# GpSimd's queue no longer drained at block ends, one power for two, and single waits for x

## What is computed

```
x = x + 0.5 * _L0_ffn_ref(_layernorm(x, axis=-1), L0_ffn_router_w, ...)
x = x + _L0_attn_ref(_layernorm(x, axis=-1), ...)
x = x + 0.5 * _L0_ffn_ref(_layernorm(x, axis=-1), ...)
...
x = x + 0.5 * _L2_ffn_ref(_layernorm(x, axis=-1), L2_ffn_router_w, ...)
x = x + _L2_attn_ref(_layernorm(x, axis=-1), ...)
x = x + 0.5 * _L2_ffn_ref(_layernorm(x, axis=-1), ...)
...
```

```
logits = jnp.einsum('td,ed->te', xf, router_w)
top_vals, top_idx = jax.lax.top_k(logits, K)
probs = jax.nn.softmax(top_vals, axis=-1)
```

## Time and profile before

| | us |
|---|---|
| median of 3 runs | 3094.78 |
| lowest and highest | 3089.35, 3095.48 |
| span of the profiled execution | 3117.8 |
| PE busy | 2339.5 (75%) |
| DVE busy | 2080.5 (67%) |
| ACT busy | 1466.0 (47%) |
| POOL busy | 919.6 (29%) |

### The profile page before, as it was taken

How to read it: one execution, slowest core, us unless ns; L and a number is a source line. 1 busy time by engine, 2 the same in 40 slices (tenths; PEclk the granted TensorE clock), 3 DMA queues, 4 the chain that set the end, 5 groups by cost and what they waited for, 6 DMA issues and landing times. The chain is left out here.

```text
span 3117.8 us, 45115 instructions
## 1 busy us (share of the span) xinstructions
PE 2339.5 (75%) x13720; PEld 1448.2 (46%) x13720; DVE 2080.5 (67%) x5273; ACT 1466.0 (47%) x3122; POOL 919.6 (29%) x975
## 2 busy tenths in 40 slices
PE   2397688839857699999899976579584975677774
PEld 2397576738834222222222234479464873222223
DVE  3465777746644799999999924456574666576775
ACT  2265311116533388888888852156332654233232
POOL 4644234434412200010101004534254441121320
PEclk9999788869979799999999988689796996799998
DMA  4122100002220400000000000022201221000000
GB/s 144 43 65 73 34 8 14 14 26 62 59 68 14 149 17 19 19 17 19 19 19 18 9 29 21 29 54 63 68 31 40 62 82 47 0 0 0 0 0 27
DMA packets 111194, 115.74 MB, mean 37 GB/s; under 512 B 21904, under 2 KB 94192, under 8 KB 110192
## 3 DMA queue, kind: packets, MB, share of 16 engines
q1 hardware_dynamic: 92080, 71.64, 8.1%
q0 software_dynamic: 17408, 35.95, 3.4%
q10 hardware_dynamic: 1472, 5.27, 0.4%
HBM read 67.55 MB, written 44.83 MB: 36 GB/s over the span
## 5 line engine op out<-in xcount | busy, mean ns | idle before, releaser
L1732 DVE TENSOR_REDUCE attn_mx<-bank 128x1 f32<-128x512 f32 x1024 | 641.3, 683 | 59.9 <-PE bank L1511 51.9
L1633 ACT ACTIVATE attn_pT<-bank 128x512 f32<-128x512 f32 x1024 | 539.8, 604 | 126.2 <-PE bank L1526 125.8
L1511 PE MATMUL bank<-attn_K,attn_Q 48*128 48x512 bf16 x1024 | 336.5, 396 | 50.5 <-DVE attn_mx L1732 29.8
L1526 PE MATMUL bank<-attn_Q,attn_K 51*128 51x512 bf16 x1024 | 331.2, 386 | 2.4 <-ACT attn_pT L1633 1.6
L1539 PE MATMUL bank<-attn_pT,attn_vb 128*32 128x512 f32 x2048 | 275.8, 610 | 19.7 <-ACT attn_pT L1633 11.8
L1692 POOL TENSOR_TENSOR attn_m_rem<-attn_m_rem,attn_m_parts 8x128 f32<-8x128 f32 x128 | 53.3, 416 | 678.1 <-ACT attn_m_parts L1646 678.1
L1511 PEld LDWEIGHTS bank<-attn_K,attn_Q 48*128 48x128 bf16 x1024 | 71.8, 94 | 376.1 <-DVE attn_mx L1732 325.1
L2391 POOL TENSOR_TENSOR mix_rS<-mix_rT,mix_S 128x512 f32<-128x512 f32 x64 | 81.5, 1277 | 270.0 <-ACT mix_gT L2372 210.2
L903 PE MATMUL bank<-mix_prod_qk,ident 128*128 128x256 f32 x512 | 123.6, 396 | 0.9 <-issue 0.9
L903 PEld LDWEIGHTS bank<-mix_prod_qk,ident 128*128 128x128 f32 x512 | 102.5, 202 | 27.1 <-issue 13.3
L2325 PE MATMUL bank<-mix_rS,mix_sel 128*128 128x512 f32 x128 | 75.7, 680 | 41.8 <-POOL mix_rS L2391 41.8
(11 more groups left out here) (610 smaller groups left out, 5910.9 us busy)
## 6 DMA issues: line engine op xcount, KB each, us to landing
ffn0a_x_ring<-xs_rows SPq DMA_DIRECT2D x72, 65.0 KB, 1.8
ffn0b_x_ring<-xs_rows SPq DMA_DIRECT2D x72, 65.0 KB, 1.9
ffn2a_x_ring<-xs_rows SPq DMA_DIRECT2D x72, 65.0 KB, 1.8
ffn2b_x_ring<-xs_rows SPq DMA_DIRECT2D x72, 65.0 KB, 1.9
w<-in_L_w ACTq DMA_DIRECT2D x2, 2048.0 KB
ffn0a_y_back<-y_rows SPq DMA_DIRECT2D x8, 512.0 KB
ffn0b_y_back<-y_rows SPq DMA_DIRECT2D x8, 512.0 KB
w<-in_L_w SPq DMA_DIRECT2D x2, 2048.0 KB
```

The source lines that it names most:

```text
L1511: nc.tensor.matmul(a_bank[n % 3][:], slot(net.Q, h, 0, KROWS)[:, qt * P:(qt + 1) * P], slot(net.K, h, 0, KROWS)[:, hf * CH:(hf + 1) * CH], ...
L1526: nc.tensor.matmul(s_bank[n % 3][:], slot(net.K, h, 0, KROWS + MROWS)[:, kt * P:(kt + 1) * P], slot(net.Q, h, 0, KROWS + MROWS)[:, hf * CH ...
L1633: nc.scalar.activation(pT[:, kt % RING, hf * CH:(hf + 1) * CH], s_bank[(n * HPB + hf) % 3][:], ACT.Exp, scale=HD ** -0.5).then_inc(exp_rea ...
L1732: nc.vector.tensor_reduce(mx[:, h % 2, qt, hf:hf + 1], a_bank[n % 3][:], AX.X, ALU.max).then_inc(a_used, 1)
```

## The change

It has three parts, and they touch all blocks, three of the four routing stages (mix0 keeps its order), and the loads.

2. In the load stage, ffn1b and decay2 one power instruction of 128x8 values (`rstd_and_grow`) takes the place of two of 128x4: the deviation of chunk `c` and the gate of chunk `c - 1`. It waits for both of its inputs. In ffn1b and decay2 it is put amid the 8 scatters of a chunk (after 4 and after 6 of them), and in all three the last gate's power is put amid the scatters of chunk 6. Two memsets (`set_joint`) are added.
3. In the load stage each chunk of `x` has a semaphore of its own and is waited for when its turn comes. The layer-0 expert weights are issued by SyncE, behind `x` and the quantized weights, no longer by ScalarE.

```diff
-        return self.enter_context(self.nc.Block())
+        return self.enter_context(self.nc.Block(no_gpsimd_drain=True))
...
+    def set_joint(self, pool):
+        nc = self.nc
+        nc.gpsimd.memset(self.bases[:], float(np.e)).then_inc(self.joint_set, 1)
+        nc.gpsimd.memset(self.exponents[:], -0.5).then_inc(self.joint_set, 1)
+        pool.wait_ge(self.joint_set, 2)
+
+    def rstd_and_grow(self, pool, c):
+
+        pool.wait_ge(self.var_ready, c + 1)
+        pool.wait_ge(self.gap_ready, c)
+        need(pool, self.xn_ready, c)
+        need(pool, self.placed, c - 1)
+        self.nc.gpsimd.tensor_tensor(self.raised[:], self.bases[:], self.exponents[:], ALU.pow).then_inc(self.rstd_ready, 1)
...
+    def grow_last(self, pool):
+        c = NCH - 1
+        pool.wait_ge(self.gap_ready, c + 1)
+        need(pool, self.placed, c)
+        self.nc.gpsimd.tensor_tensor(self.ex[:], self.bases[:, 1, :], self.gap[:], ALU.pow).then_inc(self.rstd_ready, 1)
...
             for c in range(NCH):
-                sp.dma_start(dst[:, c * TPC:(c + 1) * TPC], src[:, c * TPC:(c + 1) * TPC]).then_inc(
-                    x_loaded if c else x_first, 16)
+                sp.dma_start(dst[:, c * TPC:(c + 1) * TPC], src[:, c * TPC:(c + 1) * TPC]).then_inc(x_loaded[c], 16)
...
             for t, src_w in quantized:
                 sp.dma_start(t[:], src_w).then_inc(int_loaded, 16)
+            for t, src_w in big:
+                sp.dma_start(t[:], src_w).then_inc(w_loaded, 16)
...
-            for dst, src in big:
-                act.dma_start(dst[:], src).then_inc(w_loaded, 16)
             steps(lambda c, depth: norm.keep(act, c), lambda c: None)
...
             def body(c, depth):
-                norm.rstd_pow(pool, c)
-                if depth > 0:
-                    norm.grow(pool, c - 1)
+                if depth == 0:
+                    norm.rstd_first(pool)
+                else:
+                    norm.rstd_and_grow(pool, c)
                 if depth > 1:
                     norm.scatter(pool, c - 2)

             def finish(c):
-                norm.grow(pool, c)
-                norm.scatter(pool, c - 1)
+                norm.scatter(pool, c - 1, range(0, 2))
+                norm.grow_last(pool)
+                norm.scatter(pool, c - 1, range(2, TPC))
                 norm.scatter(pool, c)
...
             def body(c, depth):
                 if depth > 1:
                     norm.place(dve, c - 2)
+                dve.wait_ge(x_loaded[c], 16)
                 norm.stats(dve, c)
...
-                if depth == 0:
-                    dve.wait_ge(x_loaded, 16 * (NCH - 1))
-                else:
+                if depth > 0:
                     norm.weigh(dve, c - 1)
```

GpSimd's program in ffn1b, and likewise in decay2 (there with `range(0, 3)` and `range(3, TPC)` in the loop):

```diff
-            def body(c):
-                norm.rstd_pow(pool, c)
-                if norm.route and c > 0:
-                    norm.grow(pool, c - 1)
-                    norm.scatter(pool, c - 1)
...
+            norm.set_joint(pool)
+            norm.rstd_first(pool)
+            norm.rstd_and_grow(pool, 1)
+            for c in range(2, NCH):
+                norm.scatter(pool, c - 2, range(0, 2))
+                norm.rstd_and_grow(pool, c)
+                norm.scatter(pool, c - 2, range(2, TPC))
+            norm.scatter(pool, NCH - 2, range(0, 2))
+            norm.grow_last(pool)
+            norm.scatter(pool, NCH - 2, range(2, TPC))
+            norm.scatter(pool, NCH - 1)
+            norm.all_scattered(pool)
```

More of the change, by code:

```diff
@@ L149, with __init__ @@
 class Norm:
-    def __init__(self, nc, st, net, tag, dest, route, across=False, settled=False):
-        self.across, self.settled = across, settled
+    def __init__(self, nc, st, net, tag, dest, route, across=False, settled=False, joint=False):
+        self.across, self.settled, self.joint = across, settled, joint
         def sb(name, shape, dt=F32):
@@ L164, in __init__ @@
         self.shift_ready = sem("shift_ready")
-        self.ve = sb("var_eps", [P, TPC])
-        self.rstd = sb("rstd", [P, TPC])
+        if joint:
+            self.bases, self.exponents, self.raised = (sb(k, [P, 2, TPC]) for k in ("bases", "exponents", "raised"))
+            self.ve, self.rstd, self.ex, self.gap = (
+                self.bases[:, 0, :], self.raised[:, 0, :], self.raised[:, 1, :], self.exponents[:, 1, :])
+            self.joint_set = sem("joint_set")
+        else:
+            self.ve = sb("var_eps", [P, TPC])
+            self.rstd = sb("rstd", [P, TPC])
+            if route:
+                self.ex, self.gap = sb("exp", [P, TPC]), sb("gap", [P, TPC])
         self.xn = sb("xn", [P, XRING, TOPK, TPC, XCOLS] if route else [P, CH])
@@ L190, in __init__ @@
             self.scattered = [sem(f"scattered{n}") for n in range(XRING)]
+            if joint:
+                self.grown = self.rstd_ready
     def view(self, t, c, width=D):
@@ L221, in stats @@
             need(dve, self.rstd_ready, c)
+        if self.joint and c == 0:
+            dve.wait_ge(self.joint_set, 2)
         nc.vector.tensor_scalar(self.ve[:], self.mv[:, :, 1], LN_EPS, None, ALU.add).then_inc(self.var_ready, 1)
@@ L296, in weigh @@
         rows = self.xn[:, c % XRING]
-        dve.wait_ge(self.grown, c + 1)
+        dve.wait_ge(self.grown, self.grown_count(c))
         own.then(nc.vector.tensor_scalar(self.den[:], self.ex[:], 1.0, None, ALU.add))
@@ L531, in load_stage @@
     with Scope(nc) as st:
-        norm = Norm(nc, st, net, "ln0", net.xnT[0], True)
-        x_first, x_loaded = st.sem("x_first_loaded"), st.sem("x_loaded")
+        norm = Norm(nc, st, net, "ln0", net.xnT[0], True, joint=True)
+        x_loaded = [st.sem(f"x_loaded{c}") for c in range(NCH)]
         first_loaded = st.sem("first_weights_loaded")
@@ L1132, in swiglu_stage @@
     with Scope(nc) as st:
-        norm = Norm(nc, st, net, tag, dest, router is not None)
+        norm = Norm(nc, st, net, tag, dest, router is not None, joint=router is not None)
         router = router or Router()
@@ L1842, in decay_stage @@
     with Scope(nc) as st:
-        norm = Norm(nc, st, net, tag, dest, True, across=True)
+        norm = Norm(nc, st, net, tag, dest, True, across=True, joint=True)
         part = Part(nc, st, tag)
@@ L1958, in _ @@
             nc.gpsimd.memset(state[:], 0.0).then_inc(set_up, 1)
-            for n in range(NCH):
-                if n > 1:
-                    norm.scatter(pool, n - 2)
-                norm.rstd_pow(pool, n)
-                if n > 0:
-                    norm.grow(pool, n - 1)
-            norm.grow(pool, NCH - 1)
-            norm.scatter(pool, NCH - 2)
+            norm.set_joint(pool)
+            norm.rstd_first(pool)
+            norm.rstd_and_grow(pool, 1)
+            for n in range(2, NCH):
+                norm.scatter(pool, n - 2, range(0, 3))
+                norm.rstd_and_grow(pool, n)
+                norm.scatter(pool, n - 2, range(3, TPC))
+            norm.scatter(pool, NCH - 2, range(0, 2))
+            norm.grow_last(pool)
+            norm.scatter(pool, NCH - 2, range(2, TPC))
             norm.scatter(pool, NCH - 1)
```

23 lines of the change are left out of this document (13 added, 10 removed).

## The result

The kernel after takes **3026.19 us** (median of 4 runs, 3018.49 to 3029.66), the kernel before 3093.09 beside it: ratio 0.9783, 95% interval 0.9769 to 0.9797. It is 67 us faster; I had forecast 47.7, and the time lies 7 us under my range. Timed once more, with the kernel before at 3105.93 beside it, the ratio was 0.9812 (0.9797 to 0.9826), or 58 us. So the gain is some 58 to 67 us. The sign and the places of the gain were as forecast, but the sum was 10 to 20 us short.

What follows compares the result with a forecast made beforehand. No engine is full, so time was taken as a sum over 14 stages, each with its own last wait. Savings of 26.6 + 6.9 + 4.2 + 10.0 = 47.7 us gave 3094.78 - 47.7 = 3047.1 us, range 3033 to 3064.

Steps and rivals of the forecast that it cites:

- eight drains: Ends of four routing and four expert stages: skipping GpSimd's drain saves 4 x 5.25 and 4 x 1.95, 28.8 us.
- debt in decay2: Start of decay2: a drain moved behind the barrier delays GpSimd's memsets, losing 2.2 us; bounds 0 and 2.2.
- load, order and x: Load stage: earlier chunks of x, then a loop through the joint power, end the last scatter at 128.2; 6.9 us saved.
- ffn1b, order: ffn1b: the gate's power no longer waits behind 8 scatters; 3.0 us amid chunks, 1.2 at the end, 4.2 saved.
- decay2, order: decay2: less waiting for powers, 3.5 us in the middle and 6.5 at the end; 10.0 saved, bounds 3 and 17.
- the loop that I described: Load stage: joint power waits for the previous chunk's gap, the shift for the power; 13.15 us a chunk.
- The remark in brackets: Load stage: 8 scatters and two powers, 12.1 us, set the old pace, so the joint power costs time; no size given.
- when this wait goes, the third product of the chunk meets the next one: ffn1b: silu's wait replaces the power's; three middle chunks gain nothing, the others about 1.0 us each, 3.0 in all.
- the forecast 5.05: End of decay2: four of chunk 6's scatters move into GpSimd's idle before its last power, worth 5.05 us.
- I take half: Middle of decay2: of 6.5 us of waits only 3.5 were counted, since TensorE's sums stand next.
- None of the terms is a matter of the clock: Whole kernel: the 47.7 us saving was taken unchanged from the profiled execution to the median of the runs, 23.0 lower.
- my first rival: Load, ffn1b, decay2: a joint power costs no more than a single one, 1.03 us; 55.3 saved, 3039.5 us; chance 0.25.

Runs made afterwards that it cites:

- full clock on both sides: Kernel before, and kernel after with two powers everywhere, each with 3 + 3 unneeded products a chunk in ffn1b from its third chunk: ratios 0.9993 and 0.9747.
- the run with the load stage's waits alone: Kernel before with chunks of x awaited singly and expert weights behind x in the load stage; two powers, drains kept: ratio 0.9955.
- two powers in load: Kernel after, but with the two powers of a chunk kept apart in the load stage: ratio to the kernel before 0.9791.

## Why the prediction was wrong

Each term beside what it measured; for a stage the mean of the two profiles of each kernel, less 5.3 for its drain. Over four profiles of each order, ffn1b comes to 10.5 and decay2 to 12.0:

| term | forecast | measured |
|---|---|---|
| eight drains | 28.8 | 4 x 5.31 + 4 x 1.90 = 28.8 |
| debt in decay2 | -2.2 | 0 |
| load, order and x | 6.9 | 142.35 - 5.3 - 129.2 = 7.9 |
| ffn1b, order | 4.2 | 186.35 - 5.3 - 168.75 = 12.3 |
| decay2, order | 10.0 | 151.65 - 5.3 - 134.2 = 12.1 |
| sum | 47.7 | 61.1 |

- **The drains** were right, in place and in size. The debt was not: I took the worse of two bounds. GpSimd's memsets in decay2 start as early as before, and no gap came up elsewhere.
- **The load stage** went by the loop that I described. Statistics of chunk 1 at 8.06; shift to shift 12.9 us late in the stage (82.6 to 95.5; forecast 13.15 with a power of 1.85, 12.96 with the measured 1.66); last scatter issued by 127.51 (forecast 128.2). The remark in brackets, that the joint power costs time here, was worth a number: 6.3 to 6.8 us, shown by two runs.
- **ffn1b** is the large miss: 8 of the 13 us. The failed step is "when this wait goes, the third product of the chunk meets the next one", by which three chunks would gain nothing and three 1.0 us each. The third product does meet silu, but for 0.8 us in a chunk of after, and the shift goes out before it; the rows' turning, TensorE's sums and the next chunk stand behind the shift. At the full clock on both sides 3.2 us a chunk came through (18.6 to 15.4). With 3 us at half clock a chunk took 18.6 us in the old order (the run with the load stage's waits alone) and 16.9 in the new one, 1.8 less, for a wait that fell from 2.7 to 0.4. The upper bound of that term, 17.6, was on record, but I gave the range only 6 for ffn1b and decay2 together.
- **Part of ffn1b's 12.3 is the clock.** Up to the stage's last shift its half-clock time fell from 62 and 58 us to 45 and 51. In the one profile of the new order that had as much as before, 65 (two powers in load), the stage took 174.5, which is 6.6 under the 181.05 of before without the drain. So I estimate some 7 us for the waits at a like clock, and 5 that came with less half clock. That rests on one profile, and the two are not independent, since the change shortens the rests themselves.
- **decay2**: at its end the forecast 5.05 came (31.6 to 26.6 us behind the last shift). "I take half" was too little for the rest: 7.1 in place of 5.0, with some 7 us less at half clock amid the chunks (36 to 29). How much of these 2.1 us is the wait's and how much the clock's is not shown.
- **"None of the terms is a matter of the clock"** is the other step that failed, and it made the range too narrow. The same code takes 322.6 or 339.8 us in mix0 and 167.6 or 174.5 in ffn1b, with 17 and 21 us more at half clock in the longer ones. That may be why the first measurement (67 us) and the second (58) differ by as much as their intervals allow, but no run shows it. The second puts the kernel at 0.9812 x 3094.78 = 3036.6, within my range and still 10 under my 3047. I had also feared a slower clock of TensorE once it rests less. It was not slower: 0.887 and 0.892 were granted before, 0.901 and 0.892 after.
- **The skill's pages.** The Trainium skill (DMA: Bandwidth & Descriptors, Issuing engines are not separate DMA queues) says that a second issuing engine saves only sequencer time; I had left it without effect on the sum. The trace agrees for ScalarE: its first rows start at 8.18 us (forecast 8.2). The Trainium skill (GPSIMD Engine Reference, section 3.1) puts an element of GpSimd's elementwise work at about 2.6 cycles over a dispatch. Read so for a power, which it doesn't price, added columns would be nearly free, my first rival. The rows refute that reading: 4 columns take 1.01 us, 8 columns 1.66.

## What to carry to other kernels

When a wait goes, ask what goes out before the next wait comes: here the shift did, and three quarters of the wait came through (3.2 of 4.3 us at the full clock) where I had let a sixth through (3.0 of 17.6). Put a latency-bound instruction amid a long row of issues, and join two only where neither delays the other: the joint power cost 6.8 us in the one stage where its second operand came late. Profile twice before a stage's length is believed. Where TensorE rests 2 us twice a chunk, try to fill the rests, with no more work than fits. It gave 17 us in ffn1b and nothing clear in mix0.

## What the runs showed of the hardware

- **GpSimd's drain leaves nothing behind.** 5.3 us after 64 indirect DMAs were saved at each of four ends, and they show up nowhere later: the drain at the semaphore clear behind load takes 0.11 us in both kernels, a scatter 0.97 and 0.98, the store 9.7 and 9.8.
- **Useless work can pay.** 36 products of 128x512 in the rests of ffn1b keep the granted clock at 1.00 where it was 0.90 or 0.67, and a chunk falls from 16.8 or 20.4 us to 15.4. Four a chunk more in mix0 halve its half-clock time (101 to 52 us) without making the stage clearly shorter.
- **One code, several lengths of a chunk.** Chunks of ffn1b with the same instructions take 16.9 us (0.90 granted) or 20.4 (0.67). In one execution the long ones came in a row, in another they alternated with short ones.
- **The lower clock shows in the work's own length.** Where the profile has no granted clock, in the load stage, six products of 128x24 take 1.43 us, as they do at 0.51 granted, and not the 0.81 of 1.00.
